# Scattering the expert blocks' results by adding transfers into three sums in HBM, one of them holding the residual

## What is computed

```python
def body(acc, expert):
    gw, uw, dw, e = expert
    w_tok = jnp.sum(jnp.where(sel == e, rw, 0.0), axis=-1)
    h = jax.nn.silu(x @ gw.T) * (x @ uw.T)
    y = h @ dw.T
    return (acc + w_tok[:, None] * y, None)
acc0 = jnp.zeros_like(x)
out, _ = jax.lax.scan(body, acc0, (gate_w, up_w, down_w, jnp.arange(E)))
...
x = x + _L1_ffn_ref(_layernorm(x, axis=-1), L1_ffn_router_w, ...)
```

## Time and profile before

| | us |
|---|---|
| median of 3 runs | 3139.02 (3135.64 to 3144.53) |
| the profiled execution | 3125.45 |
| its span, first to last instruction | 3123.7 |
| PE busy in the span | 2545.8 (81%) |
| DVE busy | 2165.1 (69%) |
| block pass, first to last scatter issued | 2786.8 to 3051.7 |
| sums, first load issued to end of the span | 3054.26 to 3123.7 |

### The profile page before, as it was taken

One profiled execution on the slowest core, in us unless ns is written; L12 is line 12 of the kernel. 1 busy time (PEld: TensorE's weight loads), 2 busy tenths in 40 slices (PEclk: granted clock), 3 DMA queues, 4 the chain that ended last, 5 costly groups with the idle time before them and its releaser, 6 DMA issues. The chain is left out here.

```text
span 3123.7 us, 37382 instructions
## 1 busy us (share of the span) xinstructions
PE 2545.8 (81%) x11114; PEld 1319.3 (42%) x11114; DVE 2165.1 (69%) x2990; ACT 1313.0 (42%) x2141; POOL 650.0 (21%) x581
## 2 busy tenths in 40 slices
PE   4558897989788988898889889987999788649990
PEld 2114344534353444344444444344434434437770
DVE  2994888587858784888488848875788731236566
ACT  4223644364436443644364435543555321313330
POOL 2100100130313021302121212121111200235554
PEclk8779998989898988998899889988899899769995
DMA  2220231033203320232023201320133310065558
GB/s 98 101 88 12 95 104 54 19 103 106 72 20 103 102 73 23 85 118 75 23 70 115 93 23 56 113 101 31 41 108 107 112 45 26 23 180 163 163 152 332
DMA packets 119747, 275.55 MB, mean 88 GB/s; under 512 B 14288, under 2 KB 62816, under 8 KB 119408
## 3 DMA queue, kind: packets, MB, share of 16 engines
q1 hardware_dynamic: 103408, 232.20, 22.6%
q0 software_dynamic: 13824, 38.55, 3.4%
q10 hardware_dynamic: 2304, 2.20, 0.2%
HBM read 220.91 MB, written 51.98 MB: 87 GB/s over the span
## 5 line engine op out<-in xcount | busy, mean ns | idle before, releaser
L1751 PE MATMUL bank<-scan,ident 128*128 128x512 f32 x1024 | 543.5, 667 | 111.6 <-DVE scan L1221 100.5
L1212 DVE TENSOR_TENSOR_SCAN scan<-scan 128x1024 f32<-128x1024 f32 x256 | 585.6, 2287 | 60.8 <-ACT scan L963 30.3
L963 ACT ACTIVATE scan<-scan,resident 128x511 f32<-128x511 f32 x512 | 338.4, 712 | 231.1 <-DVE scan L1212 230.5
L1751 PEld LDWEIGHTS bank<-scan,ident 128*128 128x128 f32 x1024 | 200.5, 208 | 396.7 <-issue 258.1
L1221 DVE TENSOR_TENSOR scan<-scan 128x1024 f32<-128x1024 f32 x256 | 311.6, 1217 | 40.6 <-POOL g_ss L733 24.2
L1244 DVE TENSOR_TENSOR scan<-scan 128x1024 f32<-128x1024 f32 x256 | 317.9, 1242 | 28.3 <-PE bank L1751 15.7
L753 POOL DMA_INDIRECT rows_dram<-stage,slot_at x128 | 227.9, 1780 | 420.2 <-DVE scan L1212 363.5
L1385 DVE TENSOR_REDUCE rest<-bank 128x2 f32<-128x1024 f32 (+3 forms) x176 | 195.1, 1126 | 86.9 <-PE bank L1810 84.2
L1656 PE MATMUL bank<-hT,wslot 128*128 128x512 f32 x512 | 247.9, 607 | 3.3 <-PE bank L1751 2.6
L1010 ACT ACTIVATE rest<-bank 128x2048 f32<-128x2048 f32 (+3 forms) x128 | 158.1, 1235 | 172.0 <-PE bank L1830 172.0
L731 POOL TENSOR_SCALAR rs<-mv 128x4 f32<-128x4 f32 x24 | 10.1, 420 | 990.4 <-DVE off L1145 990.4
(11 more groups left out here) (275 smaller groups left out, 3931.9 us busy)
## 6 DMA issues: line engine op xcount, KB each, us to landing
scan<-bc_dram SPq DMA_DIRECT2D x256, 512.0 KB, 3.8
wslot<-wt SPq DMA_DIRECT2D x64, 384.0 KB, 3.1
rest<-rows_dram SPq DMA_DIRECT2D x160, 134.0 KB, 2.2
scan<-y_dram SPq DMA_DIRECT2D x32, 512.0 KB, 10.1
scan<-wt SPq DMA_DIRECT2D x4, 1536.0 KB, 11.5
resident<-w SPq DMA_DIRECT2D x1, 4528.5 KB, 13.3
xa<-x SPq DMA_DIRECT2D x8, 512.0 KB, 3.9
x_dram<-xb SPq DMA_DIRECT2D x8, 512.0 KB, 2.9
```

The costliest lines, as they stand in the source:

```text
L963: i = a.activation(decay[:, unit % 2, n, 1:], dt[:, c, 1:], ACT.Exp, scale=a_neg[:, c, 2 * pair + n:2 * pair + n + 1])
L1212: d.tensor_tensor_scan(flat, decay[:, unit % 2].rearrange("p n t -> p (n t)"), flat, 0.0, ALU.mult, ALU.add).then_inc(decay_used.sem, 1)
L1751: m = t_.matmul(A.bank(("y", c)), ident[:, :], drive[:, unit % NDRIVE, n], start=(pair == 0 and n == 0), stop=(pair == NPAIR - 1 and n == 1))
```

## The change

The four row sets and the residual become three sums of 4096 + 128 rows in HBM. Scatter b adds its rows to sum b mod 3 instead of writing them to rows of their own, and the residual is stored straight into sum 0. Since two adding transfers must not touch the same rows at once, POOL waits before scatter b until scatter b-3, the previous one on the same sum, has landed. Lanes without a token add to the 128 extra rows. Sums 1 and 2 and the extra rows of sum 0 are filled with zeros by three transfers from SP, issued after `scan_in(0)`. At the end three row sets are read per sequence instead of five, and DVE alone makes two adds; POOL's `sums` is gone.

```diff
+            def sums_zeroed():
+                sp.wait_ge(consts, 1)
+                zeros = lambda n: pad[:, 0:HID].unsqueeze(1).broadcast_to([P, n, HID])
+                for i in range(1, NSUM):
+                    sp.dma_start(sum_dram[i].rearrange("(t p) d -> p t d", p=P), zeros(TOKENS // P + 1)).then_inc(sums_zero, 16)
+                sp.dma_start(sum_dram[0][TOKENS:], pad[:, 0:HID]).then_inc(sums_zero, 16)
...
-                sp.dma_start(x3_dram[bass.ds(turn, 1)].rearrange("b (t p) d -> p (b t) d", p=P), xb).then_inc(out_stored.sem, 16)
+                x3 = sum_dram[0][0:TOKENS].rearrange("(b s) d -> b s d", b=BATCH)
+                sp.dma_start(x3[bass.ds(turn, 1)].rearrange("b (t p) d -> p (b t) d", p=P), xb).then_inc(out_stored.sem, 16)
...
-                        for k in range(TOPK):
-                            first = k * TOKENS + c * SEQ
-                            sp.dma_start(final[:, c % NFS, k], tokens(y_dram[first:first + SEQ])).then_inc(f_in[c % NFS], 16)
-                        sp.dma_start(final[:, c % NFS, TOPK], tokens(x3_dram[c])).then_inc(f_in[c % NFS], 16)
+                        for k in range(NSUM):
+                            sp.dma_start(final[:, c % NFS, k], tokens(sum_dram[k][c * SEQ:(c + 1) * SEQ])).then_inc(f_in[c % NFS], 16)
...
             for _ in scan_in(0):
                 pass
+            sums_zeroed()
             weave(rest_io(0), scan_in(1), ORDER["SP"])
...
-            const(g.iota(counting[:, 0:TOPK * NT], pattern=[[TOKENS, TOPK], [P, NT]], base=-int(NONE), channel_multiplier=1))
+            const(g.iota(counting[:, 0:TOPK * NT], pattern=[[0, TOPK], [P, NT]], base=-int(NONE), channel_multiplier=1))
...
             def experts_out():
+                pool.wait_ge(sums_zero, 16 * NSUM)
+                pool.wait_ge(out_stored.sem, out_stored.at(BATCH - 1, 16))
                 for b in range(NBLK):
                     pool.wait_ge(y_copied, b + 1)
-                    g.indirect_dma_start(y_dram, bass.IndirectOffsetOnAxis(ap=y_at[:, b % (2 * NYS):b % (2 * NYS) + 1], axis=0),
-                                         ys[:, b % NYS], None).then_inc(y_out[b % NYS], 16)
-
-            def sums():
-                for c in range(BATCH):
-                    pool.wait_ge(f_in[c % NFS], 16 * (TOPK + 1) * (c // NFS + 1))
-                    g.tensor_tensor(final[:, c % NFS, 2], final[:, c % NFS, 2], final[:, c % NFS, 3], ALU.add).then_inc(f_half, 1)
+
+
+                    last = b - NSUM
+                    if last >= 0:
+                        pool.wait_ge(y_out[last % NYS], 16 * (last // NYS + 1))
+                    g.indirect_dma_start(sum_dram[b % NSUM], bass.IndirectOffsetOnAxis(ap=y_at[:, b % (2 * NYS):b % (2 * NYS) + 1], axis=0),
+                                         ys[:, b % NYS], None, compute_op=ALU.add).then_inc(y_out[b % NYS], 16)
...
-                    dve.wait_ge(f_in[c % NFS], 16 * (TOPK + 1) * (c // NFS + 1))
-                    d.tensor_tensor(part[:, 0], part[:, 0], part[:, 1], ALU.add).then_inc(f_pair, 1)
-                    dve.wait_ge(f_pair, 2 * c + 1)
-                    d.tensor_tensor(part[:, TOPK], part[:, TOPK], part[:, 0], ALU.add).then_inc(f_pair, 1)
-                    dve.wait_ge(f_pair, 2 * c + 2)
-                    dve.wait_ge(f_half, c + 1)
-                    d.tensor_tensor(part[:, TOPK], part[:, TOPK], part[:, 2], ALU.add).then_inc(f_sum, 1)
+                    dve.wait_ge(f_in[c % NFS], 16 * NSUM * (c // NFS + 1))
+                    d.tensor_tensor(part[:, 1], part[:, 1], part[:, 2], ALU.add).then_inc(f_pair, 1)
+                    dve.wait_ge(f_pair, c + 1)
+                    d.tensor_tensor(part[:, 0], part[:, 0], part[:, 1], ALU.add).then_inc(f_sum, 1)
```

More of the change, by code:

```diff
@@ L48 @@
 NXS, NYS, NFS = 12, 4, 4
+NSUM = 3
 MASKED = -3.0e38
@@ L350, in build @@
         FIRST_DOWN = 28
-        final = arena[:, 0:NFS * (TOPK + 1) * NT * HID].rearrange("p (s k t d) -> p s k t d", s=NFS, k=TOPK + 1, t=NT)
+        final = arena[:, 0:NFS * NSUM * NT * HID].rearrange("p (s k t d) -> p s k t d", s=NFS, k=NSUM, t=NT)
         def in_drive(slot, n):
@@ L514, in build @@
         f_out = [sem(f"f_out{i}") for i in range(NFS)]
-        f_pair, f_half, f_sum = sem("f_pair"), sem("f_half"), sem("f_sum")
+        f_pair, f_sum, sums_zero = sem("f_pair"), sem("f_sum"), sem("sums_zero")
         bc_dram = nc.dram_tensor("bc_dram", [2 * NSTATE, SEQ], F32).ap()
         rows_dram = nc.dram_tensor("rows_dram", [DUMMY + P, ROW], F32).ap()
-        y_dram = nc.dram_tensor("y_dram", [TOPK * TOKENS + NBLK * P, HID], F32).ap()
-        x3_dram = nc.dram_tensor("x3_dram", [BATCH, SEQ, HID], F32).ap()
+        sum_dram = [nc.dram_tensor(f"sum_dram{i}", [TOKENS + P, HID], F32).ap() for i in range(NSUM)]
         def marked(name, k):
@@ L624, in sums_io @@
                     sp.wait_ge(y_out[i], 16 * (NBLK // NYS))
-                sp.wait_ge(out_stored.sem, out_stored.at(BATCH - 1, 16))
                 tokens = lambda rows: rows.rearrange("(p t) d -> p t d", p=P)
@@ L630, in sums_io @@
                             sp.wait_ge(f_out[c % NFS], 16 * (c // NFS))
-                        for k in range(TOPK):
-                            first = k * TOKENS + c * SEQ
-                            sp.dma_start(final[:, c % NFS, k], tokens(y_dram[first:first + SEQ])).then_inc(f_in[c % NFS], 16)
-                        sp.dma_start(final[:, c % NFS, TOPK], tokens(x3_dram[c])).then_inc(f_in[c % NFS], 16)
+                        for k in range(NSUM):
+                            sp.dma_start(final[:, c % NFS, k], tokens(sum_dram[k][c * SEQ:(c + 1) * SEQ])).then_inc(f_in[c % NFS], 16)
                     if c >= 2:
                         sp.wait_ge(f_sum, c - 1)
-                        sp.dma_start(tokens(out[c - 2]), final[:, (c - 2) % NFS, TOPK]).then_inc(f_out[(c - 2) % NFS], 16)
+                        sp.dma_start(tokens(out[c - 2]), final[:, (c - 2) % NFS, 0]).then_inc(f_out[(c - 2) % NFS], 16)
                 for i in range(NFS):
@@ L721, in _ @@
             const(g.tensor_copy(lane[:, :], counting[:, 0:1]))
-            const(g.iota(spare_int[:, :], pattern=[[P, NBLK]], base=TOPK * TOKENS, channel_multiplier=1))
+            const(g.iota(spare_int[:, :], pattern=[[0, NBLK]], base=TOKENS, channel_multiplier=1))
             const(g.tensor_copy(spare[:, :], spare_int[:, :]))
@@ L838, in _ @@
             experts_out()
-            sums()
         @block.scalar
```

## The result

The changed kernel is slower: 3166.07 us (median of 5 runs, 3155.82 to 3171.51) against 3137.53 us before (5 runs, 3132.65 to 3144.53), ratio 1.0104 with a 95% interval of 1.0072 to 1.0135. Forecast were 3127 us and "faster"; measured are +28.5 us between the medians. The time lies inside the stated range of 3112 to 3180, and the sign is that of rival (a).

The account below looks back on a forecast made before the run. PE was taken to set the pace of the block pass and bytes that of the sums; sums -23.5, landing +11, last scatter +0.8, zero fills 0 make -11.7 us, from 3139.0 to 3127.3 us, range 3112 to 3180.

Parts of the forecast that it names:

- rival (a): Block pass: landing typically 3.75 us or more, pick the bound instead of PE; 38 us per microsecond above 3.25; chance 0.33.
- The sums: Final stage: 8.39 of 25.17 MB less to move and shorter adds at the end, together -23.5 us.
- The zero fills: SP's transfers of 8.8 MB at the start fit a gap where the DMA engines are idle: cost 0.
- the residual's new address: Storing the residual to another address costs nothing.
- the wait for b-3: POOL's new wait before each scatter: three steps are 5.0 us, above every landing bound, so no cost by itself.
- POOL would hardly ever be released by a scatter: Block pass: scatters should hardly ever end POOL's idle time; if one does, the landing is above 5 us.
- The landing: Adding scatter, issue to landing: 3.2 us instead of 2.4, bounds 2.4 to 4.6; +11 us, and +0.8 for the last scatter.
- The time on POOL, 0.96 us, I keep: An adding scatter holds POOL for 0.96 us, as a plain one does.
- grows the landing by as much and belongs to the same range: Any longer time of a scatter on POOL only delays its landing equally, within the 2.4 to 4.6 us bounds.
- four steps of room: DVE's reuse of `ys` needs the scatter of block b-4, four steps earlier.
- the rule: Pick loop: four blocks take landing + 0.12 + 3.23 us; landings up to 3.25 us cost nothing, the whole excess above.
- 0.44 for a landing of up to 3.3 us: Chance of the forecast case, own range 3112 to 3132 us: 0.42 of it faster, 0.02 same.

Follow-up runs that it names:

- the kernel with 16 columns: The changed kernel with 16 columns of y_at instead of 8, so picks need scatters of four groups ago: ratio to before 1.0061, pass 302.4 us.
- the kernel with the memset: The kernel before with a memset of some 0.5 us on POOL after each plain scatter: ratio 1.0097, pass 287.2 us.
- the kernel with four kinds of scatter: The changed kernel with plain and adding scatters of 128 and 64 rows by turns: adding costs POOL 0.61 us more at 128 rows, 0.52 at 64.

## Why the prediction was wrong, point by point

- **The sums.** Right: -23.9 us measured for -23.5, 45.5 us for "some 46", adds of 1.23 us, DMA share 0.99.
- **The zero fills, the residual's new address, the wait for b-3.** Right at the size of the total: plain writes with all of these gave a pass of 263.9 us. That POOL would hardly ever be released by a scatter was right too, although the view names a scatter 49 times: one scatter of 160 is held up by b-3, for 0.4 us. The condition added to it, a landing above 5 us, was about right as well: that one landed after 5.6 us, and the 13 of the kernel with 16 columns after 4.9 to 5.9 us.
- **The landing.** The step that failed is "The time on POOL, 0.96 us, I keep": it is 1.56 us. Of the 1.5 us by which the landing grew, 0.6 are POOL's. The rest, 2.37 us from the end of POOL's part to the landing where it was 1.49, is 0.9 us, for which the difference of a load and a store of 512 KB had given 0.8. That this price was near is luck as far as these runs tell: none of them shows that the two have the same cause. And it was not the whole of it: I compared two transfers that do not pass through POOL at all. With the 0.9 us alone and POOL as it was, the working with means gives 2.7 + 0.9 + 0.12 + 3.23 = 6.95 us for four blocks, a pass of 276 us, and the change would still gain some 11 us (an estimate from these rows): the missed 0.6 us on POOL is what turned the sign.
- **What a longer time on POOL does.** The prediction said that it "grows the landing by as much and belongs to the same range". That left out two places. The longer time lies once more between the pick and the next scatter of that place (3.83 us instead of 3.23). With the mean landing of the trace, 4.0 us, four blocks take 4.0 + 0.12 + 3.83 = 7.95 us; 318.5 / 159 x 4 = 8.01 were measured. And it makes POOL a bound of its own, 1.86 us a block, which no rival named: removing the picks' waits left a pass of 302 us, and slower POOL with the old landing gave 287. DVE's copies to `ys` then wait for scatters 119 times, where the prediction saw four steps of room.
- **Rival (a).** Its place was right, 35 of 40 picks waited; PE's busy share fell to 0.87. Its price was not: at the 3.9 us that were measured, 38 x 0.65 + 8 = 33 us for the pass, and 53.6 came. The missing 20 us are about POOL's 0.6 us in each of 39 groups, 23 us. With POOL left alone (the pick that waits for one scatter more) the rule's 3.23 us fits, within 0.1 us in four blocks, when the mean landing goes in and not the median.
- **The chances.** 0.44 for a landing of up to 3.3 us rested on one row of plain transfers. The range from both sides (2.4 to 4.6 us) held the median landing, 3.9 us; the point in it came from a row that could say nothing about how long an adding transfer holds POOL. No chance was given to POOL as the bound.

How much of the 53.6 us belongs to POOL and how much to the landing can't be told by adding, as each alone gives a large part: 37.5 us stay with the picks freed, 43 us come from a later landing alone, 22 us from a POOL held for 1.75 us. In the changed kernel the pass follows the slower of two loops, one through POOL alone (159 x 1.86 = 296 us) and one through POOL, the transfer and the pick (7.95 us for four blocks, 316 us). Where the two loops are near each other this is too simple: in the kernel with the memset they come to 278 and some 271 us by the same working, and the pass took 287; why it is above both was not tested. That the 0.9 us of the transfer come from its packets, one a row, fits their count, the 0.74 us more that each engine is busy, and the earlier landing with 64 rows, but no run separates that from the reading of the sum, and it stays open.

## What to carry to other kernels

The adding scatter here is paid for in three places: on the engine that issues it (0.6 us more), in each DMA engine (0.74 us more), and in its landing (1.5 us more, 0.6 of them the first). Before putting it in place of a plain one, lay the pace of the stage beside the time that it holds its issuing engine, and find every wait for its landing, buffers of indices included. Where a stage is bound by bytes, first see which of them can be moved in an earlier stage whose transfers have time to spare: moving the residuals took 10.9 us out of the sums, and the pass was 2.4 us longer in the one trace of it. And where a row names what ended an idle time, compare the start with the end of the work before it: 29 of 49 "waits for a scatter" were the 0.30 us that lie between any two scatters.

## What the runs showed of the hardware that was not expected

- The same indirect transfer of 128 rows of 1 KB holds POOL for 0.96 us as a plain write and 1.56 us as an adding one. The difference is mostly fixed: 0.61 us at 128 rows and still 0.52 us at 64 in the kernel with four kinds of scatter.
- An adding scatter makes 9 packets on each DMA engine, one of 1024 bytes for each row and one of 4 bytes, where the plain one makes 3, two of 4096 bytes and one of 4, and keeps it busy for 1.11 us instead of 0.37.
- Between two transfers issued back to back by POOL lie 0.30 us in which nothing else is shown, for plain and adding ones alike.
- From the landing that POOL waits for to the start of its next scatter pass 0.73 to 0.77 us (13 scatters of the kernel with 16 columns, 6 of the one with plain writes).
